# A recurrent state-space stack on one core: the Silus before step 4, four decays ahead of them, output products beside them, and a third state buffer

## The reference

```
xz = x @ Wi.T; xin, z = split(xz)              # 256 -> 512 and 512
xin = silu(causal_conv(xin, cw, cb))           # 4 taps along time
dt_raw, B, C = split(xin @ Wx.T)               # 16, 16, 16
delta = softplus(dt_raw @ Wdt.T + bdt)
for t:  h = h * exp(delta_t * A) + (delta_t * u_t) * B_t ;  y_t = sum_n h[:, n] * C_t[n]
x = x + ((y + xin * D) * silu(z)) @ Wo.T
```

## Time and profile before

| | |
|---|---|
| median of 3 runs | 7812.48 us (7796.15 to 7815.26) |
| span of the profiled execution | 7776.4 us |
| its own time beside the span | not listed apart; the span lies 36.1 us under the median |
| PE, DVE, ACT, POOL busy | 89%, 85%, 83%, 76% of the span |
| instructions | 144083 |
| first and last scan of the stack | 501.6 and 7708.8 us |

### The profile page before, as it was taken

One profiled execution on the slowest core, in us unless ns is written; L12 is line 12 of the kernel. 1 busy time (PEld: TensorE's weight loads), 2 busy tenths in 40 slices (PEclk: granted clock), 3 DMA queues, 4 the chain that ended last, 5 costly groups with the idle time before them and its releaser, 6 DMA issues. The chain is left out here.

```text
span 7776.4 us, 144083 instructions
## 1 busy us (share of the span) xinstructions
PE 6941.0 (89%) x40063; PEld 4774.8 (61%) x40063; DVE 6640.2 (85%) x6512; ACT 6441.2 (83%) x10314; POOL 5922.7 (76%) x4917
## 2 busy tenths in 40 slices
PE   6979999899998989999899989989999999999887
PEld 4646666666666666666666666666666666666665
DVE  3258988988898898889888988988898898889888
ACT  2258888888888888888888888888888888888887
POOL 2148887788888878788878877888888788888875
PEclk9989999999999999999999999999999999999998
DMA  4111111111111111111111111111111111111112
GB/s 161 33 43 38 40 39 46 42 38 40 42 45 43 39 37 47 42 39 40 39 47 43 40 37 42 45 43 39 39 47 43 39 39 41 45 44 38 40 38 90
DMA packets 222613, 352.40 MB, mean 45 GB/s; under 512 B 43856, under 2 KB 78448, under 8 KB 221712
## 3 DMA queue, kind: packets, MB, share of 16 engines
q1 hardware_dynamic: 218048, 332.70, 14.4%
q0 software_dynamic: 3792, 10.38, 0.4%
HBM read 325.00 MB, written 17.98 MB: 44 GB/s over the span
## 5 line engine op out<-in xcount | busy, mean ns | idle before, releaser
L875 POOL TENSOR_TENSOR drive<-du,brep 128x512 f32<-128x512 f32 x4096 | 5501.3, 1373 | 735.4 <-DVE du L1115 386.2
L907 ACT ACTIVATE ps_d<-delta,cur 128x512 f32<-128x512 f32 x4096 | 2844.0, 694 | 440.6 <-DVE state L1067 421.6
L914 ACT ACTIVATE prod<-ps_r,bcT 128x512 f32<-128x512 f32 x4096 | 2810.2, 686 | 239.0 <-PE ps_r L1221 234.4
L1221 PE MATMUL ps_r<-ident,state 128*128 128x128 f32 x16384 | 2549.8, 279 | 317.2 <-ACT prod L914 174.1
L1067 DVE TENSOR_TENSOR_SCAN state<-ps_d,carry,drive 128x512 f32<-128x512 f32 x2048 | 2504.2, 1265 | 307.5 <-PE ps_r L1221 273.0
L1067 DVE TENSOR_TENSOR_SCAN state<-ps_d,drive 128x512 f32<-128x512 f32 x2048 | 2391.5, 1208 | 299.2 <-PE ps_r L1221 235.5
L1228 PE MATMUL ps_y<-ident,prod 128*128 128x128 f32 x16384 | 2464.7, 274 | 25.9 <-ACT prod L914 25.9
L1228 PEld LDWEIGHTS ps_y<-ident,prod 128*128 128x128 f32 x16384 | 1926.5, 142 | 664.3 <-issue 514.9
L1221 PEld LDWEIGHTS ps_r<-ident,state 128*128 128x128 f32 x16384 | 1832.8, 141 | 765.7 <-ACT prod L914 493.1
L1269 PE MATMUL ps_r<-xm,w_inz_sb 128*128 128x512 f32 x1024 | 507.4, 618 | 89.6 <-ACT prod L914 89.6
L1261 PE MATMUL ps_r<-xm,w_inx_sb 128*128 128x512 f32 x1024 | 508.7, 620 | 22.1 <-ACT prod L914 14.5
(11 more groups left out here) (148 smaller groups left out, 4596.3 us busy)
## 6 DMA issues: line engine op xcount, KB each, us to landing
brep<-bc_dram SPq DMA_DIRECT2D x1024, 256.0 KB, 3.2
w_sb<-w SPq DMA_DIRECT2D x8, 1024.0 KB
w_all<-w SPq DMA_DIRECT2D x8, 1024.0 KB, 11.6
xb<-xs_dram SPq DMA_DIRECT2D x39, 128.5 KB, 2.1
w_all<-x SPq DMA_DIRECT2D x4, 1024.0 KB, 9.0
w_inx_sb<-w_in SPq DMA_DIRECT2D x8, 512.0 KB, 4.0
w_inz_sb<-w_in SPq DMA_DIRECT2D x8, 512.0 KB, 4.5
w_out_sb<-w_out SPq DMA_DIRECT2D x8, 512.0 KB, 4.0
```

Of the source, the lines that this page charges most:

```text
L875: nc.gpsimd.tensor_tensor(drive[:, k % DRIVE, :], du[:, j, :], brep[:, n % BREP, :], ALU.mult).then_inc(drive_set, 1)
L907: nc.scalar.activation(ps_d[:, k % 2, :], delta[h][:, j, :], ACT.Exp, scale=cur[h][:, a:a + 1]).then_inc(decay_set, 1)
L914: nc.scalar.activation(prod[:, t, :], ps_r[:, item_place(U, h, kind, item), :], ACT.Copy, scale=bcT[(h + 1) % 2 if item[1] == "prev" else ...
L1221: last = nc.tensor.transpose(out[:, j * P:(j + 1) * P], state[n % 2][:, j, t * P:(t + 1) * P], ident[:])
```

## The change

Decays 18 to 21 of a unit (`HELD`) go to the four blocks of `soft` instead of `ps_d`. ScalarE makes them at step (4,0), and right behind them the Silus, which stood at (4,2). Behind the Silus decays run further ahead than before, by `AHEAD`, down to k + 2 again at step 32; at some steps there is none, at some two. A decay in `ps_d` waits for the last scan that used its place. The states lie in three buffers by `STATE_IN` (0, 1, 2 in turn, state 15 in 1), and a scan waits for the transposes of the state that last used its buffer. O0 and O1 both move to step (3,3), XD from (4,2) to (4,3), the second addition from (6,1) to (5,1), and the first four conv steps from (5,2), (5,2), (6,0), (6,2) to (6,0), (6,0), (6,2), (6,3). To make room, the marks of values out of range lie in `low`, a product with ones drops out of CNT, and of B and C transposed only C is kept (`cT`).

```diff
+STATE_IN = [n % 3 for n in range(STATES - 1)] + [1]
+HELD = [18, 19, 20, 21]
+AHEAD = [5, 4, 4, 4, 3, 3, 3, 3, 2, 2, 2, 2, 1, 1, 1, 1]
-RING_AT = {"CNT": (3, 0), "O0": (4, 1), "O1": (5, 3), "XD": (4, 2), "BC": (7, 3), "DT0": (6, 0), "DT1": (6, 2), "DT2": (8, 0),
+RING_AT = {"CNT": (3, 0), "O0": (3, 3), "O1": (3, 3), "XD": (4, 3), "BC": (7, 3), "DT0": (6, 0), "DT1": (6, 2), "DT2": (8, 0),
...
-SILU_AT, EXP_AT, LN_AT = (4, 2), [(7, 0), (10, 1)], [(8, 3), (11, 3)]
-MARK_AT, ALIVE_AT, ADD_AT = [(2, 1), (2, 2)], (3, 1), [(4, 3), (6, 1)]
+SILU_AT, EXP_AT, LN_AT = (4, 0), [(7, 0), (10, 1)], [(8, 3), (11, 3)]
+MARK_AT, ALIVE_AT, ADD_AT = [(2, 1), (2, 2)], (3, 1), [(4, 3), (5, 1)]
...
-CONV_AT = [(5, 2), (5, 2), (6, 0), (6, 2), (9, 2), (10, 1), (12, 2), (12, 3), (15, 1), (17, 0), (17, 3), (19, 0)]
+CONV_AT = [(6, 0), (6, 0), (6, 2), (6, 3), (9, 2), (10, 1), (12, 2), (12, 3), (15, 1), (17, 0), (17, 3), (19, 0)]
...
+def state_user(n):
+
+    return max(m for m in range(n - STATES, n) if STATE_IN[m] == STATE_IN[n])
...
-        over = sb("over_mark", [P, 2, DB, T], BF16)
+        over = low[:].rearrange("p s t -> p (s t)").bitcast(BF16).rearrange("p (s k t) -> p s k t", s=2, k=DB)
...
-        state = [sb(f"state{k}", [P, CB, T]) for k in range(2)]
+        state = [sb(f"state{k}", [P, CB, T]) for k in range(3)]
...
+        def decay(k):
+
+            return soft[:, HELD.index(k), :] if k in HELD else ps_d[:, k % 2, :]
+
+        def decays_upto(s):
+
+            ahead = AHEAD[s - 4 * SILU_AT[0]] if 0 <= s - 4 * SILU_AT[0] < len(AHEAD) else 0
+            return s + 3 + ahead
...
-                if not (is_first(U) and k < 2):
-                    act.wait_ge(scanned, TILES * U + k - 1)
+                if k not in HELD and not (is_first(U) and k < 2):
+                    act.wait_ge(scanned, TILES * U + max([m for m in range(k - 2 - len(HELD), k) if m not in HELD and (k - m) % 2 == 0]) + 1)
...
-                        k = CB * n + t + 2
-                        if k < TILES:
-                            exponent(U, h, k)
-                        elif kind != "last":
-                            exponent(U + 1, 1 - h, k - TILES)
                         if (n, t) == SILU_AT:
+                            for k in HELD:
+                                exponent(U, h, k)
...
                             nc.scalar.preload_act_table_set(TABLE)
+                        for k in range(decays_upto(CB * n + t - 1), decays_upto(CB * n + t)):
+                            if k in HELD:
+                                continue
+                            if k < TILES:
+                                exponent(U, h, k)
+                            elif kind != "last":
+                                exponent(U + 1, 1 - h, k - TILES)
...
-                nc.vector.tensor_tensor_scan(state[n % 2][:, j, :], ps_d[:, k % 2, :], drive[:, k % DRIVE, :],
+                nc.vector.tensor_tensor_scan(state[STATE_IN[n]][:, j, :], decay(k), drive[:, k % DRIVE, :],
...
-                nc.tensor.matmul(out, ones_row[:], ones_time[:], start=True, stop=False)
```

More of the change, by code:

```diff
@@ L92 @@
 READ_AT = {name: divmod(CB * n + t + 1, CB) for name, (n, t) in RING_AT.items()}
-FRONT_AT = {at: name for name, at in RING_AT.items()}
+FRONT_AT = {at: [name for name in RING_AT if RING_AT[name] == at] for at in RING_AT.values()}
 OUT_ITEMS = ["O0", "O1"]
@@ L567, in _, with kind_before @@
                 keep_y(BLOCKS - 1)
+def state_user(n):
+    return max(m for m in range(n - STATES, n) if STATE_IN[m] == STATE_IN[n])
+def kind_before(U, kind):
+    return "near" if kind == "last" else "first" if isinstance(U, int) and U == 1 else "mid"
 def ring_items(kind):
-    names = [("S", "prev" if n == 0 else n - 1, t) if k == 0 else FRONT_AT.get((n, t), FRONT_AT.get((n + STATES, t)))
-             for n in range(STATES) for t in range(TC) for k in range(2)]
+    names = [name for n in range(STATES) for t in range(TC)
+             for name in [("S", "prev" if n == 0 else n - 1, t), *FRONT_AT.get((n, t), []), *FRONT_AT.get((n + STATES, t), [])]]
     turned = [x for x in names if isinstance(x, tuple)]
@@ L581, in ring_items @@
     left = {"first": turned[:TC] + OUT_ITEMS, "mid": [], "near": EARLY_ITEMS, "last": EARLY_ITEMS + LATE_ITEMS}[kind]
-    return [x for x in names if x is not None and x not in left]
+    return [x for x in names if x not in left]
 ITEMS = {kind: ring_items(kind) for kind in ("pre0", "pre1", "first", "mid", "near", "last", "end")}
@@ L673, in mamba @@
         xdbl = sb("xdbl", [P, T])
-        bcT = [sb(f"bcT{h}", [P, TC, XD]) for h in range(2)]
+        cT = [sb(f"cT{h}", [P, TC, STATES]) for h in range(2)]
         soft = sb("soft", [P, CB, T])
@@ L860, in keep_carry @@
                 wait_counted(scanned, TILES * U + CB * n + CB)
-                nc.gpsimd.tensor_copy(carry[:, n, :], state[n % 2][:, :, T - 1]).then_inc(carried, 1)
+                nc.gpsimd.tensor_copy(carry[:, n, :], state[STATE_IN[n]][:, :, T - 1]).then_inc(carried, 1)
             def unit(U, h, it, kind):
@@ L906, in exponent @@
                     act.wait_ge(cur_in[h], loads_of(U, h))
-                nc.scalar.activation(ps_d[:, k % 2, :], delta[h][:, j, :], ACT.Exp, scale=cur[h][:, a:a + 1]).then_inc(decay_set, 1)
+                nc.scalar.activation(decay(k), delta[h][:, j, :], ACT.Exp, scale=cur[h][:, a:a + 1]).then_inc(decay_set, 1)
             def weigh(U, h, kind, item, V, n, t):
@@ L1073, in mark_over @@
                     dve.wait_ge(ring_vec, items_before(U, kind)[1])
+                if kind in ("first", "mid"):
+                    dve.wait_ge(delta_set, 2 * U + 2)
                 xs = xres[:, :, bass.ds((it % BATCH) * SEQ + h * T, T)]
@@ L1220, in turn_state @@
                 for j in range(CB):
-                    last = nc.tensor.transpose(out[:, j * P:(j + 1) * P], state[n % 2][:, j, t * P:(t + 1) * P], ident[:])
+                    last = nc.tensor.transpose(out[:, j * P:(j + 1) * P], state[STATE_IN[n]][:, j, t * P:(t + 1) * P], ident[:])
                 last.then_inc(ring_ready, 1)
@@ L1246, in count_over @@
                 if kind == "pre0":
-                    pe.wait_ge(consts_set, 3)
+                    pe.wait_ge(consts_set, 1)
                 pe.wait_ge(over_set, 2 * F + 2)
-                nc.tensor.matmul(out, ones_row[:], ones_time[:], start=True, stop=False)
                 for side in range(2):
                     for k in range(DB):
-                        last = nc.tensor.matmul(out, minus_ones[:], over[:, side, k, :], start=False, stop=(side == 1 and k == DB - 1))
+                        last = nc.tensor.matmul(out, minus_ones[:], over[:, side, k, :], start=(side == 0 and k == 0), stop=(side == 1 and k == DB - 1))
                 last.then_inc(ring_ready, 1)
@@ L1335, in unit @@
             def unit(U, h, it, kind):
-                past = "near" if kind == "last" else "first" if isinstance(U, int) and U == 1 else "mid"
+                past = kind_before(U, kind)
                 for n in range(STATES):
```

36 lines of the change are left out of this document (17 added, 19 removed).

## The result

| | before | after |
|---|---|---|
| median | 7804.31 us (7779.98 to 7815.26, 4 runs) | 8170.34 us (8154.34 to 8173.53, 4 runs) |
| span of the profiled execution | 7776.4 us | 8152.6 us |
| mean granted clock of TensorE | 0.992 | 0.954 |

The ratio is **1.048** (95% interval 1.0456 to 1.0506): slower, as forecast, by twice as much (366 us instead of 180). 8170 us lies above the range, which ended at 8130. A unit, here the distance between the first scans of units 6 and 58 divided by 52, takes 119.07 us instead of 113.11 (in the profiled executions).

The account below looks back on a forecast made before the run. Waits between engines bound the kernel, the largest VectorE's for ScalarE during the Silus, through the ring `ps_r`. Order +0.2 and port +2.7 gave 2.9 us a unit, 180 us over 62 units: 7990 us, 8-in-10 range 7680 to 8130.

Parts of the forecast that it names:

- Sign and first half: Slower (chance 0.62); waits before the first output addition and scan 20 shrink, VectorE waits 6.4 us at the first conv step.
- The walk: One even unit's timeline followed through the change: first conv step at 46.8, scan 25 at 48.1, order of work alone.
- The port: At scans 18 to 21, VectorE with two SBUF inputs and GpSimd exclude each other: +2.7 us a unit, 0 to +9.5.
- From there to scan 36: Stretch behind scan 25: three more weighings (1.75 us) before decay 35; 1.2 us later in even units, 0.2 in odd.
- The choice between `xm` and the scans: Who is held up around scans 18 to 21: turns move later work 1.6 us, or `xm` and product 22 late, 1.2.
- The order of work: Whole unit, moved work without SBUF reads: +0.2 us a unit, bounds -1.5 to +1.7.
- (a): Rival: only the order counts, no port wait for a scan, +0.2 us a unit, 7825 us; chance 0.22 with (d).
- (b): Rival: wait for X0 does not open, first conv step by about 42; 5.35 us a unit go, 7480 us; chance 0.22.
- (c): Rival: one held scan in some units lets several products pass, 5 us a unit or more, 8120 and up; chance 0.11.
- (d): Rival: decay 22, still behind the Silus, is the same wait; (a) within 0.3%; chance 0.22 with (a).

Follow-up runs that it names:

- the held scans from PSUM: Changed kernel, but scans 18 to 21 read `ps_d` instead of `soft` (wrong decays for these four tiles): 7931.15 us, ratio 1.020.
- The fillers: Changed kernel plus three zero products on TensorE at (5,3): 8065.71 us, ratio 1.038; with 16 short ones at (4,0) besides: 8087.45 us, ratio 1.037.
- XD and conv put right: Changed kernel with XD at (3,3) and the first four conv steps at (6,2), (6,2), (6,3), (7,0): 7704.22 us, ratio 0.989.
- `xm` out of the way: Changed kernel with XD at (3,3) and the later conv steps, and GpSimd's `xm` at (5,3) instead of (5,1): 7700.96 us, ratio 0.988.

## Why the prediction was wrong

**Sign and first half: right, step by step, in the even unit that was walked.** The waits for the first output product and before scan 20 went. The largest wait moved to the first conv step (forecast over 4 us and 6.4 in the walk, measured 6.8 and 6.4 in even and odd units). X0's copy comes 20.4 us after the held decays begin (4099.25 and 4119.67; forecast some 20). The walk gave the first conv step at 46.8 and scan 25 at 48.1, plus the port's 1.6 and 1.6 + 1.1: 48.4 and 50.8. It counts from 3900, though, and unit 30 of the earlier trace rows starts 0.4 later, so counted from the unit's first scan it says 48.0 and 50.4. In the changed unit 30 they start at 48.4 and 50.8, 0.4 late. That this is so near is partly luck: with the held scans from PSUM scan 25 starts at 49.4 in even units, 1.7 us later than the walk without the port had it, and the port then adds 1.5 us instead of 2.7. In odd units, which the walk took to be alike, the first conv step starts at 50.8 and scan 25 at 52.1, as XD is late there behind TensorE's gap of 3.8 us.

**The step that failed** is "From there to scan 36". It puts decay 35 some 15.0 us behind decay 27 in an even unit, by taking the 13.6 of before, adding three weighings and taking off 0.4. It measures 17.7; in an odd unit the same walk gives 14.8, and it measures 17.6. ScalarE's own work there grew by 1.8 to 1.9 us, as the three weighings said (1.75); what the walk has at nothing are 2.5 and 2.3 us in which ScalarE waits for TensorE. Of the 3.05 us that the unit (5.95 longer) has over the forecast (2.9), 2.5 arise in this stretch and 0.8 before decay 27 (0.5 in even units, 1.1 in odd ones); behind decay 35 some 0.3 come back. The walk had written down itself that VectorE stands still for 6.4 us and that decay 27 waits for scan 25 behind it; it did not go on to what ScalarE's and TensorE's standing still does to what follows, and priced DT0 and the transposes at rows taken at full clock. The fillers show the clock's share, though not its exact size. In whole kernels they won 1.3 us a unit (one) and 0.9 (two); the first leaves half of the low clock, the second has a gap of its own. An estimate from the stretches gives more: with two of them decay 27 to 35 is shorter by 1.86 us (even) and 1.82 (odd), and decay 27 of odd units comes 0.97 earlier, 2.3 us a unit on average or some 140 us over 62 units. It leaves out what that gap costs the even units. The 0.9 and 0.8 us that ScalarE still waits for TensorE at full clock are the rest of what the stretch was short of.

**The port** was sized about right: 2.7 forecast, 2.2 measured before decay 27 and 3.1 over the unit with the clock that it brings down; by itself, in the kernel before, 3.9. So the sum was near and its parts less so: 1.5 in even units and 3.0 in odd ones before decay 27. The `soft` scans last 1.9 us on average, inside the 1.8 to 3 that were given, though those of even units lie below it (1.6, and 2.3 in odd ones). The choice between `xm` and the scans went both ways: in even units `xm` took 3.32 us and scan 22 waited 2.9 for its drive, in odd units all four scans were held up. The rule of the Trainium skill, "SBUF — State Buffer", "SBUF: two separate sides", was the right one to go by: without it the forecast would have been 7825 us.

**The order of work** at +0.2 was too low: 2.8 us a unit are left when the port is taken out, 1.1 of them before decay 27 (walked: -0.1) and the rest behind it, again with the low clock (5.1 us a unit).

**The rivals.** (a) fell: the held scans are not smooth. (b) was not what happened, but its condition was the right one to name: with the first conv step no longer held up (44.8 in unit 30 with XD and conv put right, where it asked for about 42) the kernel is faster, though by 1.1% and not by 4. (c) has the time (8120 and up), by a mechanism that is rare: the longest held scan is 4.6 us, the median 1.65 or 2.2. (d) was a part of it: scan 22 waits 2.9 us in even units, for a drive and not for its decay, but with `xm` out of the way 1.6 us remain, and these end with decay 22.
